# Attention with a folded feed-forward on one core: the last unit's sums in two products, its neighbours' halves in idle query buffers, second queries among the foldings, and a new plan

## The reference

```python
xn = _layernorm(x, axis=-1)
q_blhd = jnp.einsum('bld,dhk->blhk', x_bld, Wq)
latent_bll = jnp.einsum('bld,dc->blc', x_bld, Wkv_down)
k_blhd = jnp.einsum('blc,chk->blhk', latent_bll, Wk_up)
v_blhd = jnp.einsum('blc,chk->blhk', latent_bll, Wv_up)
attn = jnp.einsum('bqhd,bkhd->bhqk', q_blhd, k_blhd) / jnp.sqrt(jnp.asarray(HD, dtype=x_bld.dtype))
attn = jax.nn.softmax(jnp.where(mask, attn, neg_inf), axis=-1)
y_blhd = jnp.einsum('bhqk,bkhd->bqhd', attn, v_blhd)
return jnp.einsum('bqhd,hdo->bqo', y_blhd, Wout)
h = jnp.einsum('btc,cd->btd', x, weight)
h = jnp.einsum('btc,cd->btd', h, aux_weight1)
h = jnp.einsum('btc,cd->btd', h, aux_weight2)
return jnp.tanh(h + bias)
```

## Time and profile before

| | |
|---|---|
| runs (three) | 1958.02, 1958.07, 1961.17 us; median 1958.07 |
| profiled execution | 1955.77 us, of which the span of instructions is 1954.1 |
| mean granted TensorE clock | 0.999 |
| PE, PEld busy | 1930.8, 1310.7 us |
| DVE, ACT, POOL busy | 1366.3, 1143.7, 1456.2 us |

### The profile page before, as it was taken

One profiled execution on the slowest core, in us unless ns is written; L12 is line 12 of the kernel. 1 busy time (PEld: TensorE's weight loads), 2 busy tenths in 40 slices (PEclk: granted clock), 3 DMA queues, 4 the chain that ended last, 5 costly groups with the idle time before them and its releaser, 6 DMA issues.

```text
span 1954.1 us, 38790 instructions
## 1 busy us (share of the span) xinstructions
PE 1930.8 (99%) x13536; PEld 1310.7 (67%) x13536; DVE 1366.3 (70%) x3626; ACT 1143.7 (59%) x2201; POOL 1456.2 (75%) x1277
## 2 busy tenths in 40 slices
PE   8999999999999999999999999999999999999998
PEld 7667666667666666666666667666666666666664
DVE  7778666787578766698666967658567795666662
ACT  5565655656565655665556556556565565665562
POOL 1778678777787877887677887787777867788782
PEclk9999999999999999999999999999999999999999
DMA  5122121321222121231112212122121221222110
GB/s 144 46 72 61 53 56 47 83 56 53 53 62 76 50 56 53 59 85 53 45 48 71 73 48 61 53 69 64 47 67 45 83 58 37 61 61 58 42 45 28
DMA packets 117599, 116.50 MB, mean 60 GB/s; under 512 B 24092, under 2 KB 100764, under 8 KB 117404
## 3 DMA queue, kind: packets, MB, share of 16 engines
q1 hardware_dynamic: 117404, 114.02, 21.5%
HBM read 53.67 MB, written 8.91 MB: 32 GB/s over the span
## 4 chain that ended last, share of the span: by engine, by line
PE 92%; DVE 6%; issue 1%; ACT 1%; DMA 1%; POOL 0%; SPq 0%; ACTq 0%; DVEq 0%; POOLq 0%
PE ps L1074 25%; PE ps L999 21%; PE ps L1092 14%; PE ps L1056 13%; PE ps L1059 13%; PE ps L1119 3%; DVE split_lo L1369 1%; DVE ps L1329 1%; PE ps L1105 1%; DVE maxima L1334 1%; PE ps L1151 1%; DMA probs<-in_L_attn_Wq 0%; PE ps L1032 0%; DVE x_in L1434 0%; PE ps L1173 0%
## 5 line engine op out<-in xcount | busy, mean ns | idle before, releaser
L1494 POOL TENSOR_TENSOR p_sum<-p_sum,probs 128x512 f32<-128x512 f32 x660 | 850.6, 1319 | 133.7 <-ACT probs L1229 132.7
L1229 ACT ACTIVATE probs<-ps 128x512 f32<-128x512 f32 x1152 | 660.5, 597 | 300.4 <-PE ps L1059 282.3
L1329 DVE CUSTOM_DVE_ANT_0 ps<-ps,causal 128x512 f32<-128x512 f32 (+4 forms) x1024 | 521.3, 527 | 229.2 <-PE ps L1092 221.3
L1074 PE MATMUL ps<-probs,latent 128*32 128x512 f32 x4608 | 518.1, 594 | 0.3 <-DVE q_lo L1457 0.3
L1092 PE MATMUL ps<-k_hilo,q_hi 128*128 128x512 f32 (+4 forms) x1536 | 481.7, 356 | 5.9 <-DVE maxima L1329 1.9
L1056 PE MATMUL ps<-q_hi,k_hilo 128*128 128x512 f32 x1152 | 467.8, 406 | 1.8 <-ACT probs L1229 0.8
L1059 PE MATMUL ps<-q_lo,k_ones 65*128 65x512 f32 x1152 | 457.1, 397 | 0.0
L1334 DVE TENSOR_REDUCE maxima<-ps 128x1 f32<-128x512 f32 (+1 forms) x512 | 326.0, 637 | 152.8 <-PE ps L1092 148.2
L1494 POOL TENSOR_TENSOR p_sum<-probs 128x512 f32<-128x512 f32 x222 | 288.3, 1314 | 164.0 <-ACT probs L1229 159.1
L1074 PEld LDWEIGHTS ps<-probs,latent 128*32 128x32 f32 x4608 | 139.0, 110 | 316.3 <-issue 312.3
L1092 PEld LDWEIGHTS ps<-k_hilo,q_hi 128*128 128x128 f32 x1536 | 281.4, 189 | 100.0 <-issue 21.9
(11 more groups left out here) (110 smaller groups left out, 2258.8 us busy)
## 6 DMA issues: line engine op xcount, KB each, us to landing
q_hi<-q_hi SPq DMA_DIRECT2D x256, 128.0 KB, 2.4
norm<-recips SPq DMA_DIRECT2D x254, 128.0 KB, 2.9
q_lo<-q_lo SPq DMA_DIRECT2D x128, 128.0 KB, 2.4
x_in<-in_L_attn_x_bld SPq DMA_DIRECT2D x16, 512.0 KB, 4.6
acc<-in_L_attn_x_bld SPq DMA_DIRECT2D x32, 256.0 KB, 2.9
out_x<-acc SPq DMA_DIRECT2D x64, 128.0 KB, 1.7
q_lo<-rows SPq DMA_DIRECT2D x128, 4.0 KB
rows<-norm SPq DMA_DIRECT2D x127, 4.0 KB
```

What stands on the lines that cost most here:

```text
L1074: last = nc.tensor.matmul(y_bank[row:row + WIDTH, :], latent[par][:, key_block(unit, s), half:half + WIDTH], probs[:, t % PT_SLOTS, g * BA ...
L1229: nc.scalar.activation(probs[:, t % PT_SLOTS, g * BANK:(g + 1) * BANK], ps[:, bank_of[kind, key], :], ACT.Exp).then_inc(exp_done, 1)
L1329: nc.vector.tensor_tensor_reduce(bank, bank, causal[:, BANK - w:BANK], 1.0, LOWEST, ALU.add, ALU.max, maxima[:, unit % 4, h, 0:1]).then_in ...
L1494: nc.gpsimd.tensor_tensor(sums, other, probs[:, slot, part], ALU.add).then_inc(pool_done, 1)
```

## The change

**The last unit's sums.** POOL now adds the probabilities of unit 127 too, for all steps but the last. `R` then is two products: ones by `p_sum`, and ones by the last step's probabilities, 16 matmuls in all. The planner may place `R` before the last PVs. `DV` keeps only the reciprocal; the multiplication is `DM`, which reads `y` straight from PSUM after the last PV. ACT's copy of that `y` is gone.

**Halves of the last four units.** `split_of` gives units 124 to 127 a slot each, in the query buffers of half 61, which nothing uses any more. Their `HI` no longer waits for the `O` of the unit before.

**The beginning.** `Wq` is loaded in two pieces, the first ahead of `Wk_up`, and is turned ahead of it in two parts. "fold wqk 0" comes before the first transposes of `xn`, which come all together. "casts" moves from DVE to POOL. The first keys wait for the low halves of their own side only. Q (1, 0) and Q (1, 1) move in among "fold wvo" and the last maxima, and "fold wff" behind `MT`; banks are assigned anew.

**The plan.** 24 rules for segments of 24 steps replace 16 rules for segments of 36. The smallest batch of PVs was 10 in eleven of the sixteen, and 4, 6 and 7 (three times) in the others; it is now 10 in fifteen, 8 in eight and 4 in one. Maxima were to go 11 steps ahead in most segments and now go 9 to 15. The planner's start values for free banks and ready queries differ, so its whole order can differ.

```diff
-SEGMENT = 36
+SEGMENT = 24
 RULES = [
-    (7, 11, 0, 1.5, 300, 600, 0),
-    (7, 11, 0, 1.5, 300, 600, 0),
-    (10, 11, 0, 1.0, -300, 2000, 800),
...
-    (10, 11, 0, 0.5, 0, 600, 300),
+    (4, 10, 0, 0.5, 0, 2000, 300),
+    (8, 9, 0, 2.5, 0, 1200, 0),
...
-        self.q_ready = {(0, 0): 0.0, (0, 1): 0.0, (1, 0): 1000.0, (1, 1): 4500.0}
-        self.bank_free = [0.0, 0.0, 0.0, 3500.0, 1500.0, 1000.0, 1000.0, 1000.0]
+        self.q_ready = {(n, j): 0.0 for n in range(2) for j in range(2)}
+        self.bank_free = [0.0, 0.0, 0.0, 2500.0, 2000.0, 3000.0, 3500.0, 4000.0]
...
-                self.multiplied[key] = self.run("DVE", when, (2200, 2300))
-                if key[0] - 1 in self.out:
-                    self.after(self.multiplied[key], "HF", key)
+                self.run("DVE", when, (1760, 1860))
+            elif kind == "DM":
+                self.after(self.run("DVE", when, (340, 440)), "HF", key)
...
+        if self.sums and self.sums[0][1] == self.units - 1:
+            out.append((max(self.masked[-4:]), now - 9, self.place_r))
...
-            return self.split.get(("TL", (key[0], 1, 1)))
+            return self.split.get(("TL", (key[0], 1, key[1])))
...
-        added = s > 0 and u < self.units - 1
+        added = s > 0 and (u < self.units - 1 or s < block_of(u))
...
-            done = self.on_pe("R", ready, PE_TIME["PV"])
+            self.takes("MAX", "R", u)
+            done = self.on_pe("R", ready, (1720, 1930))
             for part in range(2):
-                self.after(max(done, self.y_copied[u]) + part, "DV", (u, part))
+                self.after(done + 2 * part, "DV", (u, part))
+                if self.n_pv == len(self.steps):
+                    self.after(done + 2 * part + 1, "DM", (u, part))
...
-    plan += [("LN4", (0, k)) for k in range(2)] + [("W", "turn wk"), ("W", "turn wq")]
-    plan += [("T", (0, c, 0)) for c in range(2)] + [("LN4", (0, k)) for k in range(2, 4)]
-    plan += [("TL", (0, c, 0)) for c in range(2)] + [("W", "casts"), ("W", "fold wqk 0")]
-    plan += [("T", (0, c, 1)) for c in range(2)] + [("TL", (0, c, 1)) for c in range(2)]
+    plan += [("LN4", (0, k)) for k in range(4)]
+    plan += [("W", "turn wq 0"), ("W", "turn wk"), ("W", "turn wq 1"), ("W", "fold wqk 0")]
...
+    for side in range(2):
+        plan += [("T", (0, c, side)) for c in range(2)] + [("TL", (0, c, side)) for c in range(2)]
     plan += [("W", "fold wqk 1")]
     for side in range(2):
         plan += [*two_parts("K", (0, side)), ("KL", (0, side))]
     plan += [*two_parts("Q", (0, 0)), ("QL", (0, 0)), *two_parts("Q", (0, 1)), ("QD", (0, 0))]
...
-    plan += [("W", "fold aux"), *maxima[2:5], ("W", "fold wvo"), *maxima[5:], ("W", "fold wff")]
-    plan += [("MT", 0), ("W", "split wvo"), *two_parts("Q", (1, 0)), *two_parts("Q", (1, 1))]
-    plan += [("QL", (1, 0)), ("QD", (1, 0)), ("XA", 0), ("XA", 1), ("XA", 2)]
-    plan += [("QL", (1, 1)), ("QD", (1, 1))]
-    bank, n_p0, n_max = {}, 0, 0
+    plan += [("W", "fold aux"), *maxima[2:5], *two_parts("Q", (1, 0)), ("W", "fold wvo")]
+    plan += [*maxima[5:], *two_parts("Q", (1, 1)), ("QL", (1, 0)), ("MT", 0), ("W", "fold wff")]
+    plan += [("QL", (1, 1)), ("W", "split wvo"), ("QD", (1, 0)), ("QD", (1, 1))]
+    plan += [("XA", 0), ("XA", 1), ("XA", 2)]
+    bank, n_max = {}, 0
+    p0_banks = iter((6, 0, 1, 5, 6, 0, 1, 6, 0, 0, 1))
...
+                (wq_in[:, :, 0:4 * P], wq_rows[:, :, 0:4 * P], wq_loaded[0]),
                 (wk_in, Wk_up.rearrange("c h k -> c (h k)"), wk_loaded),
-                (wq_in, Wq.rearrange("(c p) h k -> p c (h k)", p=P), wq_loaded),
+                (wq_in[:, :, 4 * P:8 * P], wq_rows[:, :, 4 * P:8 * P], wq_loaded[1]),
...
+            both = [slice(r * LATENT, (r + 1) * LATENT) for r in range(2)]
+            pool.wait_ge(wkv_loaded, 16)
+            for cols in both:
+                nc.gpsimd.tensor_copy(wkv_hi[:, :, cols], wkv_in).then_inc(consts_made, 1)
+            pool.wait_ge(consts_made, 10)
+            for cols in both:
+                nc.gpsimd.tensor_tensor(wkv_lo[:, :, cols], wkv_in, wkv_hi[:, :, cols].bitcast(F32),
+                                        ALU.subtract).then_inc(consts_made, 1)
...
+                    if c == 0 and j in (0, 4, 6):
+                        pe.wait_ge(w_copied, max(4, 3 + j // 2))
...
-            elif what == "casts":
-                dve.wait_ge(wkv_loaded, 16)
-                for cols in both:
-                    nc.vector.tensor_copy(wkv_hi[:, :, cols], wkv_in).then_inc(w_split, 1)
-                dve.wait_ge(w_split, 8)
-                for cols in both:
-                    nc.vector.tensor_tensor(wkv_lo[:, :, cols], wkv_in,
-                                            wkv_hi[:, :, cols].bitcast(F32),
-                                            ALU.subtract).then_inc(w_split, 1)
...
+        def split_of(unit, final):
+
+            if unit >= final - 3:
+                n = 2 * (final - unit) % 4
+                free = (q_hi if unit >= final - 1 else q_lo)[(final // 2 - 2) % Q_BUFS]
+                free = free[:, :, :].rearrange("p (n j) q -> p n (j q)", n=4)
+                return free[:, n, :], free[:, n + 1, :]
+            return split_hi[:, unit % SPLIT_SLOTS, :], split_lo[:, unit % SPLIT_SLOTS, :]
...
-                    if unit == final and s < block_of(unit):
-                        if s == 0:
-                            take_bank("R", unit)
-                        broadcast_sums(t, s == 0, False)
...
-                    broadcast_sums(first_step(key) + block_of(key), False, True).then_inc(p1_full, 1)
+                    bank, last_step = take_bank(kind, key), first_step(key) + block_of(key)
+                    wait_new(pool_done, 2 * last_step)
+                    broadcast_sums(bank, lambda part: p_sum[:, key % SUM_SLOTS, part], True, False)
+                    wait_new(exp_done, 2 * last_step + 2)
+                    broadcast_sums(bank, lambda part: probs[:, last_step % PT_SLOTS, part], False,
+                                   True).then_inc(p1_full, 1)
...
-                elif kind == "PV" and key[2] == block_of(key[1]):
+                elif kind == "PV" and key[1] < final and key[2] == block_of(key[1]):
...
-                    if key >= SPLIT_SLOTS:
+                    if SPLIT_SLOTS <= key < final - 3:
                         act.wait_ge(p1_full, count.p1("O", key - SPLIT_SLOTS) + 1)
-                    nc.scalar.activation(split_hi[:, key % SPLIT_SLOTS, :], y[:, key % Y_SLOTS, :],
+                    elif key == final - 3:
+                        act.wait_ge(st_full, 2 * HALF_STEPS * (final // 2 - 1))
...
+                elif kind == "DM":
+
+                    unit, part = key
                     dve.wait_ge(last_divided, 2 * part + 1)
-                    nc.vector.tensor_tensor(y[:, slot, cols], y[:, slot, cols], norm[:, slot, cols],
+                    if part == 0:
+                        dve.wait_ge(pv_done, first_step(unit) + block_of(unit) + 1)
+                        dve.wait_ge(norm_lo, unit - Y_SLOTS + 1)
+                    slot, cols = unit % Y_SLOTS, half_bank(part)
+                    nc.vector.tensor_tensor(y[:, slot, cols], norm[:, slot, cols],
+                                            ps[:, bank_of["Y", unit], cols],
                                             ALU.mult).then_inc(last_divided, 1)
...
-                if unit == final:
+                if unit == final and s == block_of(unit):
```

More of the change, by code:

```diff
@@ L260, in flush @@
                 self.multiplied[key] = self.run("POOL", when, (1300, 1350))
-                if key < SPLIT_SLOTS or key - SPLIT_SLOTS in self.out:
+                if key == 0 or (key - SPLIT_SLOTS in self.out if key < self.units - 4
+                                else key - 1 in self.halved):
                     self.after(self.multiplied[key], "HI", key)
             elif kind == "HI":
+                self.halved.add(key)
+                if key >= self.units - 5 and key + 1 in self.multiplied:
+                    self.after(max(when, self.multiplied[key + 1]), "HI", key + 1)
                 self.after(self.run("ACT", when, ACT_TIME[kind]), "LO", key)
@@ L384, in place_p1_half @@
         self.out[u] = done
-        for part in range(2):
-            if (u + 1, part) in self.multiplied:
-                self.after(max(done, self.multiplied[u + 1, part]) + part, "HF", (u + 1, part))
-        if u + SPLIT_SLOTS in self.multiplied:
+        if u + SPLIT_SLOTS in self.multiplied and u + SPLIT_SLOTS < self.units - 4:
             self.after(max(done, self.multiplied[u + SPLIT_SLOTS]), "HI", u + SPLIT_SLOTS)
@@ L471, in place_pvs @@
                 self.takes("Y", "Y", u)
+            final = u == self.units - 1 and s == block_of(u)
             self.plan.append(("PV", (t, u, s)))
@@ L474, in place_pvs @@
             self.pv.append(end)
-            if u == self.units - 1 and s < block_of(u):
-                if s == 0:
-                    self.takes("MAX", "R", u)
```

(25 more changed lines are left out.)

116 lines of the change are left out of this document (63 added, 53 removed).

## The result

The kernel became slower: 1964.69 us median (1963.29 to 1968.73, 11 runs) against 1958.06 for the kernel before, a ratio of 1.0038 with an interval of 1.0029 to 1.0047. That is +6.6 us where -11.3 was predicted. The mean granted clock is 0.992 in this profile and 0.999 in that of the kernel before, while the medians over the executions of the two kernels are 0.994 and 0.997: the part that the clock has in the two profiles is larger than its part in the +6.6.

The account below looks back on a forecast made before the run. PE's own work was taken to bound the middle, with a serial tail at the end. End -8.3, beginning -2.0 and new plan -1.0 summed to -11.3 us: 1946.8 us for the median, range 1940.5 to 1954.

Parts of the forecast that it names:

- The new plan: Middle of the kernel: the new order of steps was taken to give -1 us, with a range of -8 to +8.
- edges: Start and finish of the kernel, outside the middle: their changes were together to give -10.3 us.
- rival 5: Middle: new order doubles or triples PE's waits, slower from 22 us of waits, 1963.8 at 24 us; chance 0.07.
- priced it once (0.7) at the end: Last matmuls before the output: 0.7 us added for PE running slower after being idle 3 us or more.
- The end: Last units: less PE work on sums and a shorter serial tail were to give -8.3 us.
- the POOL route: Last unit: POOL's additions, ending at 1933.7, then the sums' products to 1935.4, were to decide when the reciprocals start.
- rival 2: Tail: a `LO` held up by POOL, or POOL late by as much, 5 us less gain, 1951.8; chance 0.15.
- The beginning: Before the body: earlier keys, -1.0 us, and 1.0 of a 1.5 us wait before the first maxima; -2.0 together.
- the wait of 1.51: Before the body's first maxima: PE's idle of 1.51 us was to go, of which 1.0 was counted as gain.
- The fold of `wff` covers the row's DMA of unit 0 as the queries did: Start of the body: PE's folding work was to hide unit 0's row transfer, so no wait was counted for it.
- the lock as one instruction's wait (2.0 us): Tail: reading by which a `LO` meeting POOL waits for one instruction only, 2.0 us, and the full -8.3 stays.

## Why the prediction was wrong

**The step that failed** is "The new plan": "I take -1 and keep -8 and +8 for the range". It is +13.3 beside the new edges and +20.3 alone. Its mechanism stood in the text as rival 5, at 0.07: more `LO` caught with PE behind them. I had the earlier trace rows in hand and asked only which `LO` the *added* POOL work could catch at the end. But seven of 127 were already caught, and only one of them, the longest, reached PE, by 2.48 us. Which of them reach PE depends on the order, and the order was made anew. After: eleven over 3 us, three of them with PE behind by 3.75 to 4.69 us, and one, of 6.03 us from 375.4, by 1.07 us through the work that stood behind it on DVE.

**What a catch costs was also too small.** The price was the wait. The stretch at the lower clock behind it adds an estimated 2.2, 3.3 and 2.9 us in the profile; I had such a case in the earlier trace rows, priced it once (0.7) at the end, and never in the middle. So rival 5's point of decision, 22 us of waits, was wrong as well: 14.13 in the middle were enough, with one catch behind 1829, 8.4 us of clock, and edges worth 7 instead of 10.3. That its 1963.8 lies near the measured 1964.69 is luck, since it adds up other terms. After the four catches are taken away (1948.87) the new order is level with the old one with its own catch taken away (1947.85; the intervals overlap). That is the evidence that most of what the order costs is its catches. It is not a proof that it costs nothing else: the two kernels take them away by different edits, and with the same edit the new order is 5.4 slower, with catches left. Why POOL has a long run ready just at units 93, 109, 122 and 123 was not traced; the planner has a fixed cost for each of DVE's operations and none for meeting POOL.

**The end**: -5.4 alone against -8.3. Right: 16 matmuls of sums, `DM` 0.42, the POOL route, the distance from first reciprocal to last addition. Mis-sized: POOL starts 2.3 later, waits twice for exponentials and ends 2.8 later, and the sums run 1.9 longer at the lower clock. Within the whole change rival 2 came too: `LO` of unit 122 at 12.83 us, longer than any row of before. POOL then adds for unit 127 until 1950.1, 16 us later than forecast, the last ten additions without a pause; two `NM` queue behind them, and all three last `O` come after the sums:
```profile
1936.73 13.39 POOL L1532 TENSOR_TENSOR p_sum<-p_sum,probs 128x512 f32<-128x512 f32 x10
1950.06 2.53 POOL L1507 TENSOR_TENSOR y<-y,norm 128x512 f32<-128x512 f32 x2
...
1953.07 1.74 DVE L1379 RECIPROCAL norm<-ps 128x256 f32<-128x256 f32 x1
...
1958.14 0.36 PE L1026 MATMUL ps<-wvo_hi,q_hi 128*128 128x256 f32 x1 [3.18 <-DVE q_hi L1408]
```
**The beginning**: -1.4 against -2.0. Keys came at 17.5 in the changed kernel (forecast 18.3), and the wait of 1.51 is gone, as said. "The fold of `wff` covers the row's DMA of unit 0 as the queries did" is refuted by the 1.70 us above; I had counted Q (1, 1) on PE and its DMAs past the loads, but not its copies on ACT and its DMAs on SP ahead of the row. The granted clock is 0.50 for 6.8 us from 41.9 behind it, with 6.5 us of PE's work in it, so an estimated 3.2 us are lost there, which the sum had nowhere.

Two slips of the text decide nothing: 1950.98 less 1942.6 is 8.4 and not 8.3, and by the cases the chances are 0.13 for the same time and 0.07 for slower.

On how long a loser waits, the row kept me from reading the lock as one instruction's wait (2.0 us), and 12.83 us bears the row out. The Trainium skill, "SBUF — State Buffer", section "SBUF: two separate sides", says that whichever side starts first has the pair "for the whole instruction"; here the other side waited through some ten POOL operations in a row, so in this trace the wait did not end with one instruction.

## What to carry to other kernels

When an order is made anew, list the instructions that another engine can hold up, however harmless they are today, and price each as if the critical engine stood behind it; a planner without that term places them without regard to it. Price a stall of TensorE with the slower clock after it. And where two engines exclude each other, a single wait that makes the long queue pause for the short instruction can be worth more than the whole change around it: four gave 15.8 us here.

## What was not expected of the hardware

- DVE's subtraction with two SBUF inputs waits through a whole run of POOL operations: 12.83 us beside additions, masks and products begun from 1911.63 to 1925.2. It ended 0.55 us after POOL's last one, here, in the one from 1484.47 and in the one from 1728.79.
- The stretch at the lower clock does not follow each wait. In the profile of the changed kernel it lasts 6.8 us after waits of 1.70, 3.75, 4.33 and 4.69, and there is none behind the wait of 3.18 at 1954.96, after which PE's pieces of `O` take 0.28 us as at full clock. In the kernel with unit 122 alone held off, the same wait of 3.75 has 3.4 us of it.
- One kernel does not get the same clock each time: 23 executions of the kernel before have mean granted clocks from 0.995 to 0.999; the four lowest took 1959.4 to 1961.1 us, the five highest 1953.9 to 1957.4.
- A wait of one length at one place had no such stretch in the kernel before (2.48 us at 1479) and one of 3.4 us in the kernel with the new end alone (2.46 us there) and in the one with both new edges (2.48).
- A catch can move: with unit 122 held off, unit 123 was caught, for 6.22 us of wait and some 1.8 of clock against 4.69 and 2.9, and the time stayed where it was.
